# Start-up loads, the openings of two attention stages and one matmul order in a sixteen-stage network

## The chip, the core and the metric

The kernel runs on one core of a Trainium2 chip. The metric is the device time of one execution in microseconds (us), as the median of several; lower is better. The core has five engines with a queue of instructions each: TensorE (PE; its weight loads are the rows PEld), VectorE (DVE), ScalarE (ACT), GpSimd (POOL) and SyncE (SP, which here issues most DMAs). The engines meet only at semaphores: an instruction raises one when it is done (`then_inc`), and another engine's queue waits for a value of it (`wait_ge`).

## The reference, cut to what matters

Sixteen layers in a row, each `x = x + layer(layernorm(x))`, over a batch of 4 blocks of 512 positions with 128 features. The layers that the change touches compute this:

```python
# L0 and L3 "attn_a" (Mamba): conv of 4 taps over time, then a scan over time with 16 states
xc = sum(x_pad[:, k:k + Lln, :] * conv_w[:, k] for k in range(D_CONV)) + conv_b
h = A_bar * h + dt_t[..., None] * B_t[:, None, :] * x_t[..., None]
# L0 and L2 "attn_b" (narrow attention): 16 heads of 8 features, softmax over all keys (L2: causal)
score = softmax(einsum('bhif,bhjf->bhij', q, k) / SCALE); attn = einsum('bhij,bhjf->bihf', score, v)
# L1 "ffn": weights given as booleans, +1 or -1
w = jnp.where(kernel_bool, 1.0, -1.0)
# L1 "attn_b" (wide attention): 16 heads of 64 features, softmax, output projection
logits = einsum('bhne,bhme->bhnm', q, k); out = einsum('bhnm,bhme->bnhe', softmax(logits), v)
# L3 "attn_b" (ReLU attention): one score per head and position, standardised over time, then
# context of i = 2 * sum_j relu(z_i - z_j) * v_j / norm, by sorting in the reference
# L3 "ffn": integer weights, times 1/127
h = jax.nn.silu(gate) * up
```

## The kernel before, in words

The loop `Fori` in `network` runs two passes, each over two of the four blocks (`NB = 2`). Features lie on the 128 partitions, the 512 positions of a block along the free axis; `g.xs` holds x for both blocks through a whole pass. A pass is a chain of stages (`L0a`, `L0f`, ... `L3g`), each a `Block` of its own: no engine begins a stage before all of them have ended the one before. Within a stage the order on each engine is written out by hand. Banks 0 to 7 of `g.ps` are PSUM.

- `prepare` (L139) loads all 15,793 weight columns in eight pieces on SP, then the booleans and the integers, and on DVE makes the ternary matrix (L167 to L178), the +1/-1 matrices `g.conn` (L182 to L187) and the scaled integers `g.gated` (L192, L194). POOL folds the input projection into the conv taps of both Mamba layers in place (L207) and halves their output matrices (L208). 
- `load_x` and `store_x` (L220, L233) are stages of their own around a pass: one DMA of two blocks each, waited for.
- `mamba` begins with the norms on ACT and DVE; the first convolution (L985) follows the prepared input `xin`.
- `narrow_attention` (L0b, L2b) cuts q and k in bf16 parts. For each group of heads it first finds the row maxima: PE makes a score tile (`top_scores`, L1536), DVE takes its maximum (L1737; causal L1734). 17 such steps make a unit of a block and four heads (the 17th turns the maxima, L1530). Three PSUM banks go round: a score tile waits until DVE has done the one three before. Beside that run 64 slots: PE makes the real scores (`scores`, L1549), ACT their exponential (L1649), and in every second slot PE multiplies with the values (`products`, L1566). Each slot also holds 2 or 3 of the maxima's score tiles.
- `wide_attention` (L1b) projects k, q and v for a pair of heads (L1832, L1835), and in 64 steps makes scores (L1846), maxima on DVE (L1979), exponentials on ACT (L1942), transposes on PE (L1857) and products (L1869); the output projection of a block is L1889. All projections pass through one bank, `SMALL`, so that each waits for ACT to have copied the one before.
- `relu_attention` (L3b) makes z for queries and keys of both blocks (x = 2b the queries, 2b + 1 the keys), standardises it, cuts the queries in three bf16 parts (`split_q`), and then in 8 units u spreads four query rows over all partitions (`spread`, L2153), copies them (ACT, L2265), and makes relu(z_i - z_j) for four key tiles, three on DVE (L2415) and one on ACT (L2285), which PE multiplies with the values (L2197). Units 0 to 3 are block 0, units 4 to 7 block 1.

## Time and profile before

| | |
|---|---|
| median of 3 runs | 3164.71 us (3163.57 to 3168.61) |
| the profiled execution | 3165.05 us, its span 3163.5 us |
| PE busy | 2570.9 us (81%) |
| DVE busy | 1586.3 us (50%) |
| ACT busy | 1446.3 us (46%) |
| POOL busy | 677.6 us (21%) |
| DMA | 55.68 MB, 18 GB/s on average |

The span is the time from the first to the last instruction that the profiler recorded; what lies around it is 1.55 us here. In a row of the timeline the number in front is the start in us from the span's start, the second the duration; "x4" is how many instructions the row merges, and the bracket says how long the engine had been idle before it and what ended that.

### The profile page before, as it was taken

How to read it: one execution, taken by the hardware profiler on the slowest of the kernel's cores; microseconds unless marked ns; L12 is line 12 of the kernel's file. 1: busy time of each engine (PE TensorE's matmuls, PEld its weight loads, DVE VectorE, ACT ScalarE, POOL GpSimd, SP SyncE). 2: the span in 40 equal slices, each digit the busy share in tenths (PEclk: the TensorE clock that was granted, in tenths of full speed). 3: DMA queues.
4: the chain of work that ended last, by engine and by line, in shares of the span. 5: the costliest groups of instructions: out<-in, count | busy, mean ns of one | idle time of the engine just before them, and what ended most of it. 6: DMA issues, size and time to landing. Idle time of an engine off the chain costs nothing. (4 is left out here: it accounts for less than half of the span.)

```text
span 3163.5 us, 33520 instructions
## 1 busy us (share of the span) xinstructions
PE 2570.9 (81%) x11730; PEld 1095.1 (35%) x11738; DVE 1586.3 (50%) x2507; ACT 1446.3 (46%) x2392; POOL 677.6 (21%) x644
## 2 busy tenths in 40 slices
PE   3777788999789789768767787889997897897677
PEld 1231244544344234223222213445443442342232
DVE  3967543555121631695649585245442117217955
ACT  3544614555334354554545355155552444445454
POOL 1732010000001521371227311000000024115520
PEclk9898989999979899899889989999998898998998
DMA  3002000000010210000000010000000102100000
GB/s 122 1 1 73 8 1 1 1 1 1 1 53 1 76 59 0 0 1 1 1 15 1 25 56 1 1 1 1 1 1 0 53 1 81 54 0 1 0 1 7
DMA packets 36751, 55.68 MB, mean 18 GB/s; under 512 B 7648, under 2 KB 19936, under 8 KB 36576
## 3 DMA queue, kind: packets, MB, share of 16 engines
q1 hardware_dynamic: 32224, 49.53, 4.8%
q10 hardware_dynamic: 4352, 3.94, 0.4%
q8 instruction: 96, 1.57, 0.2%
q14 instruction: 79, 0.65, 0.1%
HBM read 39.54 MB, written 13.63 MB: 17 GB/s over the span
## 5 line engine op out<-in xcount | busy, mean ns | idle before, releaser
L522 POOL TENSOR_TENSOR xs<-xs,L2f_part 128x512 f32<-128x512 f32 x32 | 40.5, 1264 | 1181.8 <-DVE L2f_part L511 1181.8
L1942 ACT ACTIVATE L1b_pr<-ps,L1b_mneg 128x512 f32<-128x512 f32 x256 | 173.7, 684 | 197.0 <-DVE L1b_mneg L1981 197.0
L1979 DVE TENSOR_REDUCE L1b_m<-ps 128x2 f32<-128x1024 f32 x128 | 156.8, 1225 | 114.9 <-PE ps L1846 111.2
L1649 ACT ACTIVATE L0b_pt<-ps 128x1024 f32<-128x1024 f32 x128 | 129.3, 1024 | 117.9 <-PE ps L1549 115.8
L90 ACT ACT_TABLE_LOAD x44 | 56.5, 1283 | 268.0 <-PEq L224 41.4
L1737 DVE TENSOR_REDUCE L0b_mx<-ps 128x1 f32<-128x512 f32 x256 | 159.0, 684 | 37.0 <-PE ps L1536 35.5
L1226 POOL TENSOR_TENSOR L3a_db<-L3a_du,L3a_bs 128x1024 f32<-128x1024 f32 x64 | 150.4, 2360 | 114.0 <-DVE L3a_du L1337 68.1
L1226 POOL TENSOR_TENSOR L0a_db<-L0a_du,L0a_bs 128x1024 f32<-128x1024 f32 x64 | 150.5, 2359 | 112.5 <-DVE L0a_du L1337 66.0
L2005 DVE COPY L1b_prt<-ps 128x512 f32<-128x512 f32 x128 | 88.5, 692 | 124.9 <-PE ps L1857 124.6
L1354 DVE TENSOR_TENSOR_SCAN L0a_hs<-ps,L0a_db 128x1024 f32<-128x1024 f32 x64 | 146.1, 2283 | 5.4 <-ACT ps L1149 5.4
L1354 DVE TENSOR_TENSOR_SCAN L3a_hs<-ps,L3a_db 128x1024 f32<-128x1024 f32 x64 | 146.1, 2282 | 5.0 <-ACT ps L1149 5.0
L1846 PE MATMUL ps<-L1b_k,L1b_q 64*128 64x512 f32 x512 | 145.3, 646 | 0.0
L115 PE MATMUL ps<-xs,weights 128*128 128x512 f32 x128 | 79.5, 753 | 78.8 <-PEq L224 31.3
L1869 PE MATMUL ps<-L1b_prt,L1b_v 128*64 128x512 f32 x512 | 136.7, 614 | 4.1 <-issue 2.0
L1857 PE MATMUL ps<-weights,L1b_pr 128*128 128x128 f32 x1024 | 135.8, 275 | 3.0 <-ACT L1b_pr L1942 3.0
L1649 ACT ACTIVATE L2b_pt<-ps 128x1024 f32<-128x1024 f32 (+3 forms) x128 | 86.9, 706 | 105.5 <-PE ps L1549 104.8
L1857 PEld LDWEIGHTS ps<-weights,L1b_pr 128*128 128x128 f32 x1024 | 115.6, 141 | 50.6 <-issue 43.5
L1036 PE MATMUL ps<-L0a_hc,weights 128*128 128x512 f32 x256 | 127.5, 625 | 5.1 <-ACT L0a_du L1129 3.0
L511 DVE SCALAR_TENSOR_TENSOR L2f_part<-ps,weights,L2f_masks 128x512 f32<-128x512 f32 x32 | 24.1, 752 | 206.0 <-PE ps L443 206.0
L1036 PE MATMUL ps<-L3a_hc,weights 128*128 128x512 f32 x256 | 123.2, 608 | 5.1 <-ACT L3a_du L1129 3.0
L511 DVE SCALAR_TENSOR_TENSOR L2g_part<-ps,weights,L2g_masks 128x512 f32<-128x512 f32 x32 | 24.1, 752 | 202.0 <-PE ps L443 202.0
L1734 DVE CUSTOM_DVE_ANT_0 L2b_unmasked<-ps,weights 128x128 bf16<-128x128 f32 (+3 forms) x256 | 110.0, 488 | 30.4 <-PE ps L1536 27.3
(566 smaller groups left out, 5274.2 us busy)
## 6 DMA issues: line engine op xcount, KB each, us to landing
L2f_w<-expert_dram SPq DMA_DIRECT2D x32, 256.0 KB, 3.0
L2g_w<-expert_dram SPq DMA_DIRECT2D x32, 256.0 KB, 3.0
weights<-w_dram SPq DMA_DIRECT2D x7, 987.5 KB, 10.7
L0b_qs<-stack_dram SPq DMA_DIRECT2D x32, 96.0 KB, 2.2
stack_dram<-L0b_cut SPq DMA_DIRECT2D x24, 128.0 KB, 2.1
L2b_qs<-stack_dram SPq DMA_DIRECT2D x32, 96.0 KB, 2.2
stack_dram<-L2b_cut SPq DMA_DIRECT2D x24, 128.0 KB, 2.2
L0b_ks<-stack_dram SPq DMA_DIRECT2D x28, 96.0 KB, 2.2
```

What stands on the lines that cost most here:

```text
L1036: mm = pe.matmul(g.ps[:, SUM + k, :], g.w("ident"), hc[:, n % DEEP, k, :], start=(s == 0), stop=(s == NS - 1))
L1226: pool.tensor_tensor(db[:, n % DEEP, :, :], du[:, b, :, :], bcast(bs[:, n % DEEP, :], 1, 2), ALU.mult).then_inc(input_ready, 1)
L1354: dve.tensor_tensor_scan(flat(hs), decay_banks(n).rearrange("p k t -> p (k t)"), flat(db), 0.0, ALU.mult, ALU.add).then_inc(scanned, 1)
L1649: act.activation(pt[:, n % 3, 2 * half:2 * half + 2, q0:T], g.ps[:, 2 * (s % 2):2 * (s % 2) + 2, q0:T], ACT.Exp).then_inc(prob, 1)
L1734: dve.tensor_tensor_reduce(unmasked[:, e % 3, 0:span(t)], g.ps[:, bank, 0:span(t)], g.w("causal_row", T - span(t)), 1.0, -3e38, ALU.add, A ...
L1737: dve.tensor_reduce(mx[:, u, col:col + 1], g.ps[:, bank, 0:T], AX.X, ALU.max).then_inc(top_in, 1)
L1846: mm = pe.matmul(g.ps[:, 2 * (s % 2) + h, :], q[HE * h:HE * h + HE, u % 3, t * P:(t + 1) * P], k[HE * h:HE * h + HE, u % 3, :], start=True ...
L1857: mm = pe.transpose(g.ps[:, 4 + h, j * P:(j + 1) * P], pr[:, s % 2, h, j * P:(j + 1) * P], g.w("ident"))
L1869: mm = pe.matmul(g.ps[HE * h:HE * h + HE, PV, :], v[:, u % 4, j, HE * h:HE * h + HE], prt[:, u % 2, h, j, :], start=(j == 0), stop=(j == K ...
L1942: act.activation(pr[:, s % 2, h, :], g.ps[:, 2 * (s % 2) + h, :], ACT.Exp, bias=mneg[:, s % 2, h:h + 1], accum_out=total[:, u % 2, t, h:h ...
L1979: dve.tensor_reduce(m[:, s % 2, :], g.ps[:, 2 * (s % 2):2 * (s % 2) + 2, :], AX.X, ALU.max).then_inc(max_raw, 1)
L2005: dve.tensor_copy(prt[:, u % 2, 0, :, t * P:(t + 1) * P], g.ps[:, 4, :].rearrange("p (j c) -> p j c", c=P)).then_inc(turned_dve, 1)
```

## The change

What is different now, in five parts:

1. **Start.** The weights are sorted by need. SP loads 1013 columns, then x of the first pass, then 3551 columns (the rest that layer L0a needs), then the others in six pieces, which only the second stage waits for. The conversion of the booleans moves to POOL in L1a, that of the integers to POOL in L1b; both are done in each pass. The folding of the taps moves to POOL at the start of each Mamba stage, into the memory of `dt`'s second block.
2. **Turn.** `load_x` and `store_x` go. The last stage, L3g, puts its result in `g.xn` and issues for each block the store and the load of the next x into `g.xs`. A stage `close` without work stands at the end of a pass.
3. **Wide attention.** The six opening projections go to different banks; the first three wait for the first block's norm alone, and `scores(0)` comes after three of them. The last output projection goes to bank 4 and begins before the last pair is ready.
4. **ReLU attention.** Banks are spread; the queries and keys of block 0 are standardised in one instruction each, with the square of the queries on DVE; the rest of block 1's preparation is moved from between the units to before the first, and `spread(4)` from unit 2 to the end of unit 3.
5. **Narrow attention.** In a slot, the maxima's score tiles come before the products.

The diff, cut to its core:

```diff
-                for c in range(cut):
-                    a, z = c * step, min(n, (c + 1) * step)
-                    sp.dma_start(g.weights[:, a:z], wd[:, a:z]).then_inc(loaded, 16)
-                sp.dma_start(bools[:, :], boold).then_inc(bools_in, 16)
-                sp.dma_start(ints[:, :], intd).then_inc(ints_in, 16)
+                sp.dma_start(g.weights[:, 0:cut[0]], wd[:, 0:cut[0]]).then_inc(loaded, 16)
+                sp.dma_start(g.xs[:, :, :], x_dram[0:NB, :, :].rearrange("b p t -> p b t")).then_inc(x_loaded, 16)
+                sp.dma_start(g.weights[:, cut[0]:cut[1]], wd[:, cut[0]:cut[1]]).then_inc(loaded, 16)
+                for c in range(REST):
+                    a, z = (cut[1] + (n - cut[1]) * k // REST for k in (c, c + 1))
+                    sp.dma_start(g.weights[:, a:z], wd[:, a:z]).then_inc(g.rest_loaded, 16)
+                sp.wait_ge(x_loaded, 16)
...
-                dve.wait_ge(loaded, 16 * cut)
+                dve.wait_ge(loaded, 32)
...
+                dve.tensor_scalar(g.s2x[:, :], g.w("f1_s", 0, 2), 2.0, None, ALU.mult).then_inc(consts, 1)
+                dve.tensor_copy(g.cb[:, :], g.w("bf_consts")).then_inc(consts, 1)
...
-            @block.gpsimd
-            def _(pool):
-                pool.wait_ge(loaded, 16 * cut)
-                for name in ("m0", "m3"):
-                    rows = g.w(name + "_taps").rearrange("p (j e) -> p j e", j=4)
-                    pool.tensor_tensor(rows, rows, bcast(g.w(name + "_in", 0, 2 * P), 1, 4), ALU.mult).then_inc(taps, 1)
-                    pool.tensor_scalar(g.w(name + "_out"), g.w(name + "_out"), 0.5, None, ALU.mult).then_inc(taps, 1)
...
+                if last:
+                    for b in range(NB):
+                        sp.wait_ge(added, b + 1)
+                        sp.dma_start(out_dram[bass.ds(i * NB + b, 1), :, :].rearrange("b p t -> (b p) t"), g.xn[:, b, :]).then_inc(stored, 16)
+                        sp.dma_start(g.xs[:, b, :], x_dram[bass.ds(NB + b - i * NB, 1), :, :].rearrange("b p t -> (b p) t")).then_inc(x_loaded, 16)
...
-                    dve.tensor_tensor(g.xs[:, b, :], g.xs[:, b, :], g.ps[:, 4 * b + 3, :], ALU.add).then_inc(added, 1)
+                    dve.tensor_tensor(result[:, b, :], g.xs[:, b, :], g.ps[:, 4 * b + 3, :], ALU.add).then_inc(added, 1)
...
+                pool.wait_ge(bools_in, 16)
+                pool.tensor_copy(g.conn[:, :], bools[:, FF:]).then_inc(conn_steps, 1)
...
+                pool.tensor_tensor(g.conn[:, 0:FF], ahead[:, :], g.conn[:, 0:FF], ALU.subtract).then_inc(conn_steps, 1)
...
+                pool.tensor_scalar(g.conn[:, FF:], g.conn[:, FF:], 2.0, 1.0, ALU.mult, ALU.subtract).then_inc(conn_steps, 1)
...
+                        pe.wait_ge(folded, 2)
...
+                        mm = pe.matmul(g.ps[:, CONV[b] + f, :], taps[:, j, f * P:(f + 1) * P], xin[:, b, j:j + T], start=(j == 0), stop=(j == 3))
...
+                rows = g.w(w + "_taps").rearrange("p (j e) -> p j e", j=4)
+                pool.tensor_tensor(taps[:, :, :], rows, bcast(g.w(w + "_in", 0, 2 * P), 1, 4), ALU.mult).then_inc(folded, 1)
+                pool.tensor_scalar(out_w[:, :], g.w(w + "_out"), 0.5, None, ALU.mult).then_inc(folded, 1)
...
-                    if s >= LAG and (s - LAG) % 2 == 0:
-                        products((s - LAG) // 2)
                     for a in range(tops_before(s), tops_before(s + 1)):
                         top_scores(e, a)
                         e += 1
+                    if s >= LAG and (s - LAG) % 2 == 0:
+                        products((s - LAG) // 2)
                     c = (s - TURN) // 16
...
+        OPENING = (SMALL, PV, 4, 5, SMALL, PV)
+        def proj_bank(u, j):
+            return OPENING[3 * u + j] if u < 2 else SMALL
...
+                pool.wait_ge(ints_in, 16)
+                pool.tensor_copy(g.gated[:, :], ints[:, :]).then_inc(gated_steps, 1)
...
+                pool.tensor_scalar(g.gated[:, :], g.gated[:, :], 1.0 / 127.0, None, ALU.mult).then_inc(gated_steps, 1)
...
+                        else:
+                            pe.wait_ge(proj_in, 3 + h)
...
+                    if b == NB - 1:
+                        bank = LAST
...
+                    else:
+                        pe.wait_ge(at_ready, PAIRS * (b + 1))
...
+                        mm = pe.matmul(g.ps[:, bank, :], g.w("w1_wp", p * P, P), at[:, b % 2, p, :], start=(p == 0), stop=(p == PAIRS - 1))
...
 
+                pe.wait_ge(ln.done, 1)
+                for j in range(3):
+                    project(0, j)
+                scores(0)
+                project(1, 0)
                 pe.wait_ge(ln.done, NB)
-                for u in range(2):
-                    for j in range(3):
-                        project(u, j)
-                scores(0)
                 for s in range(STEPS):
                     u, t = s // KT, s % KT
                     if s + 1 < STEPS:
                         scores(s + 1)
+                    if s == 0:
+                        project(1, 1)
+                        project(1, 2)
...
-                for u in range(2):
-                    for j in range(3):
-                        take(u, j)
+                for j in range(3):
+                    take(0, j)
+                take(1, 0)
                 exps(0)
+                take(1, 1)
+                take(1, 2)
...
-                    if x >= 2:
-                        pe.wait_ge(turned_in, x - 1)
...
+                    if x == 2:
+                        pe.wait_ge(v_in, 2)
...
-                    if x == 1:
-                        pe.wait_ge(z_in, 1)
...
-                    pe.wait_ge(z_ready, b + 1)
-                    pe.wait_ge(z_in, 2 * b + 2)
+                    pe.wait_ge(k_ready, b + 1)
+                    pe.wait_ge((v_in, hid_in)[b], (1, XS)[b])
...
-                turn(3)
-                hide(2)
-                hide(3)
                 turn_keys(0)
...
-                        pe.wait_ge(turned_in, XS)
                         pe.wait_ge(hid_in, 2)
+                        pe.wait_ge(z_in, 2)
...
+                turn(3)
+                hide(2)
+                hide(3)
+                scores(2)
+                scores(3)
                 spread(1)
                 for n in range(4 * UN):
                     b, i, t = n // 16, n // 4 % 4, n % 4
-                    if n == 2:
-                        scores(2)
-                        scores(3)
-                    if n == 11:
+                    if n == 15:
+                        spread(4)
                         turn_keys(1)
-                    if t == 2 and n // 4 + 2 < UN:
+                    if n == 16:
+                        spread(5)
+                    if t == 2 and n // 4 + 2 < UN and n // 4 not in (2, 3):
                         spread(n // 4 + 2)
...
+                    if n == 8:
+                        pe.wait_ge(z_in, XS)
...
-                    act.wait_ge(z_c, x + 1)
-                    act.activation(ln.xc[:, x % 2, :], z[:, x, :], ACT.Square, accum_out=sums[:, x, 1:2]).then_inc(z_sq, 1)
...
+                    act.activation(ln.xc[:, x % 2, :], z[:, x, :], ACT.Square, bias=minus[:, x:x + 1], accum_out=sums[:, x, 1:2]).then_inc(z_sq, 1)
...
-                square(0)
...
-                take_turned(3)
-                gelu(2)
-                gelu(3)
...
+                take_turned(3)
+                gelu(2)
+                gelu(3)
+                take_z(2)
+                take_z(3)
+                load_exp_ln(g.nc)
...
-                    if u + 1 < UN:
+                    if u + 1 < UN and u != 3:
                         take_q(u + 1)
+                    if u == 1:
+                        square(2)
+                        square(3)
...
-                    if u == 0:
-                        take_z(2)
-                        take_z(3)
-                        load_exp_ln(g.nc)
                     if u == 1:
-                        square(2)
-                        square(3)
                         inverse_std(1)
-                    if u == 2:
+                    if u == 3:
+                        take_q(4)
                         take_keys(1)
...
+                def scale_k(b):
+                    x = 2 * b + 1
...
+                    pool.tensor_scalar(z[:, x, :], z[:, x, :], minus[:, x:x + 1], std[:, b:b + 1], ALU.add, ALU.mult).then_inc(k_ready, 1)
...
-                        pool.tensor_scalar(z[:, 1, :], z[:, 1, :], std[:, 0:1], None, ALU.mult).then_inc(z_ready, 1)
...
                     pool.wait_ge(z_in, x + 1)
-                    pool.tensor_scalar(sums[:, x, 2:3], sums[:, x, 0:1], 1.0 / T, None, ALU.mult).then_inc(z_mean, 1)
...
-                    pool.tensor_scalar(z[:, x, :], z[:, x, :], sums[:, x, 2:3], None, ALU.subtract).then_inc(z_c, 1)
-                pool.wait_ge(z_sq, 4)
+                    pool.tensor_scalar(minus[:, x:x + 1], sums[:, x, 0:1], -1.0 / T, None, ALU.mult).then_inc(z_mean, 1)
+                pool.wait_ge(z_sq, 3)
                 pool.tensor_tensor(var[:, 1:2], sums[:, 2, 1:2], sums[:, 3, 1:2], ALU.add).then_inc(z_var, 1)
-                pool.wait_ge(z_std, 2)
-                for x in (3, 2):
-                    pool.tensor_scalar(z[:, x, :], z[:, x, :], std[:, 1:2], None, ALU.mult).then_inc(z_ready, 1)
-                split_q(pool, z_ready, 1)
+                split_q(pool, 1)
+                pool.wait_ge(lo, 2)
+                scale_k(1)
...
-                centre_z(1)
+                mean_z(0)
+                dve.wait_ge(z_mean, 1)
+                dve.tensor_scalar(ln.xc[:, 0, :], z[:, 0, :], minus[:, 0:1], None, ALU.add).then_inc(z_c, 1)
...
+                dve.tensor_tensor_reduce(ln.sq[:, 0, :], ln.xc[:, 0, :], ln.xc[:, 0, :], 1.0, 0.0, ALU.mult, ALU.add, sums[:, 0, 1:2]).then_inc(q_sq, 1)
+                mean_z(1)
                 take_rows(2)
-                dve.wait_ge(z_sq, 2)
+                dve.wait_ge(z_sq, 1)
+                dve.wait_ge(q_sq, 1)
                 dve.tensor_tensor(var[:, 0:1], sums[:, 0, 1:2], sums[:, 1, 1:2], ALU.add).then_inc(z_var, 1)
+                scale_q(0)
+                split_q(dve, 0)
                 take_rows(3)
                 take_v(1)
-                dve.wait_ge(z_std, 1)
-                dve.tensor_scalar(z[:, 0, :], z[:, 0, :], std[:, 0:1], None, ALU.mult).then_inc(q_ready, 1)
...
-                split_q(dve, q_ready, 0)
...
-                    if u % 4 == 2:
+                    if u == 1:
+                        scale_q(1)
+                    if u == 2 or u == 5:
...
-            load_x(g, x_dram, i)
...
+    first = ("f0_w", "f0_alpha", "f0_b", "f1_s", "bf_consts", "mean_mat", "m0_alog", "m3_alog")
+    early = first + ("centre", "ident", "eps5", "eps6")
+    rank = lambda name: 0 if name in first else 1 if name in early or name.startswith("m0_") else 2
+    parts.sort(key=lambda part: rank(part[0]))
+    cut = [sum(m.shape[1] for name, m in parts if rank(name) <= k) for k in range(2)]
```

On PE, in the slots of L0b, L1536 (now L1532) are the maxima's score tiles, L1549 (L1545) the real scores and L1566 (L1562) the products. Before:

```order
L1549 MATMUL ps<-L0b_qs,L0b_ks 128x512 x2
L1566 MATMUL ps<-L0b_pt,L0b_vpad 32x512 x4
L1536 MATMUL ps<-L0b_ks,L0b_qs 128x512 x2
L1549 MATMUL ps<-L0b_qs,L0b_ks 128x512 x2
L1536 MATMUL ps<-L0b_ks,L0b_qs 128x512 x2
L1549 MATMUL ps<-L0b_qs,L0b_ks 128x512 x2
L1566 MATMUL ps<-L0b_pt,L0b_vpad 32x512 x4
L1536 MATMUL ps<-L0b_ks,L0b_qs 128x512 x2
```

Now:

```order
L1545 MATMUL ps<-L0b_qs,L0b_ks 128x512 x2
L1532 MATMUL ps<-L0b_ks,L0b_qs 128x512 x2
L1562 MATMUL ps<-L0b_pt,L0b_vpad 32x512 x4
L1545 MATMUL ps<-L0b_qs,L0b_ks 128x512 x2
L1532 MATMUL ps<-L0b_ks,L0b_qs 128x512 x2
L1545 MATMUL ps<-L0b_qs,L0b_ks 128x512 x2
L1532 MATMUL ps<-L0b_ks,L0b_qs 128x512 x2
L1562 MATMUL ps<-L0b_pt,L0b_vpad 32x512 x4
```

The four products of a slot stand behind the two score tiles where they stood ahead of them.

On PE, in the opening of L1b, L1832 and L1835 (now L1847 and L1850) are projections, L1846 (L1861) scores and L1857 (L1874) transposes of the exponentials. Before:

```order
L1832 MATMUL ps<-xn,weights 128x512 x2
L1835 MATMUL ps<-weights,xn 128x128 x4
L1832 MATMUL ps<-xn,weights 128x512 x2
L1835 MATMUL ps<-weights,xn 128x128 x4
L1846 MATMUL ps<-L1b_k,L1b_q 128x512 x4
L1857 MATMUL ps<-weights,L1b_pr 128x128 x8
```

Now:

```order
L1847 MATMUL ps<-xn,weights 128x512 x2
L1850 MATMUL ps<-weights,xn 128x128 x4
L1861 MATMUL ps<-L1b_k,L1b_q 128x512 x2
L1847 MATMUL ps<-xn,weights 128x512
L1861 MATMUL ps<-L1b_k,L1b_q 128x512 x2
L1847 MATMUL ps<-xn,weights 128x512
L1850 MATMUL ps<-weights,xn 128x128 x4
L1874 MATMUL ps<-weights,L1b_pr 128x128 x8
```

The first scores stand behind three projections instead of six, and the other three stand around the second.

On PE, in the opening of L3b, L2103 (now L2133) turn the rows, L2109 (L2141) and L2116 (L2146) are the two layers behind z, L2123 (L2153) turns the keys, L2153 (L2180) spreads queries and L2197 (L2231) are products. Before:

```order
L2094 MATMUL ps<-weights,L3b_xm 128x128 x4
L2103 MATMUL ps<-weights,L3b_rows 128x128 x8
L2109 MATMUL ps<-L3b_rt,weights 128x512 x2
L2123 MATMUL ps<-weights,L3b_z 128x16 x4
L2153 MATMUL ps<-L3b_zc,cb 128x512 x8
L2197 MATMUL ps<-L3b_re,L3b_vpad 32x512 x8
L2116 MATMUL ps<-L3b_hid,weights 128x512 x2
L2153 MATMUL ps<-L3b_zc,cb 128x512 x4
```

Now:

```order
L2126 MATMUL ps<-weights,L3b_xm 128x128 x4
L2133 MATMUL ps<-weights,L3b_rows 128x128 x4
L2153 MATMUL ps<-weights,L3b_z 128x16 x4
L2180 MATMUL ps<-L3b_zc,cb 128x512 x4
L2133 MATMUL ps<-weights,L3b_rows 128x128 x4
L2141 MATMUL ps<-L3b_rt,weights 128x512 x2
L2146 MATMUL ps<-L3b_hid,weights 128x512 x2
L2180 MATMUL ps<-L3b_zc,cb 128x512 x4
L2231 MATMUL ps<-L3b_re,L3b_vpad 32x512 x8
```

The first spread of queries stands ahead of the fourth turn and the hidden layers; the second-layer matmuls of block 1 stand before the first product instead of in the first unit.

## Rows read from the trace of the kernel before

**Rows 1.** Windows: busy us and count per engine, granted clock, DMA share, GB/s
```profile
560.00:760.00 200.00, 197.87 (x1118) 99.97 (x1117) 108.78 (x169) 115.02 (x286) 0.00 (x0) 1.00 0.00 1
265.60:351.50 85.90, 69.31 (x419) 15.30 (x418) 68.97 (x116) 53.76 (x54) 5.88 (x18) 0.94 0.15 43
```

**Rows 2.** Timeline of the start: start us, us, engine line op, idle before
```profile
0.80 4.14 SPq L159 DMA_DIRECT2D weights<-w_dram  x8
...
22.55 0.29 DVE L167 TENSOR_REDUCE prep_absum<-weights 128x1 f32<-128x128 f32 x1 [22.55 <-DMA weights<-w_dram]
...
28.08 1.98 DVE L182 CAST conn<-prep_bools 128x3072 f32<-128x3072 uint8 x1
...
39.93 3.60 PE L115 MATMUL ps<-xs,weights 128*128 128x512 f32 x4 [16.45 <-PEq L224]
...
50.16 8.77 PE L985 MATMUL ps<-L0a_xin,weights 128*128 128x512 f32 x16 [4.82 <-DVE L0a_xin L1283]
```

**Rows 3.** DMA issues of the first 40 us: count, KB each, median us to landing
```profile
weights<-w_dram SPq DMA_DIRECT2D x7, 987.5 KB, 10.7
...
xs<-x_dram SPq DMA_DIRECT2D x1, 512.0 KB, 3.7
```

**Rows 4.** Timeline of the turn between the two passes
```profile
1591.03 0.69 DVE L378 TENSOR_TENSOR xs<-xs,ps 128x512 f32<-128x512 f32 x1 [1.89 <-PE ps L354]
1592.92 0.41 SPq L239 DMA_DIRECT2D out_dram<-xs  x1
1601.30 0.42 SPq L229 DMA_DIRECT2D xs<-x_dram  x1
...
1605.85 1.28 ACT L90 ACT_TABLE_LOAD   x1 [24.68 <-PEq L224]
```

**Rows 5.** Timeline of the wide stage's opening (L1b)
```profile
501.80 1.13 PE L1832 MATMUL ps<-xn,weights 128*128 128x512 f32 x2 [2.55 <-DVE xn L136]
...
516.26 2.68 PE L1846 MATMUL ps<-L1b_k,L1b_q 64*128 64x512 f32 x8
...
520.43 1.32 PE L1857 MATMUL ps<-weights,L1b_pr 128*128 128x128 f32 x8 [1.49 <-ACT L1b_pr L1942]
```

**Rows 6.** Window of that opening
```profile
504.00:518.00 14.00, 11.25 (x28) 5.48 (x28) 0.00 (x0) 2.99 (x5) 0.00 (x0) 0.51 0.00 0
```

**Rows 7.** Timeline of the wide stage's end
```profile
782.49 7.13 PE L1889 MATMUL ps<-L1b_at,weights 128*128 128x512 f32 x16 [1.22 <-DVE L1b_at L1987]
```

**Rows 8.** Maxima of the narrow stages, engine idle until: L0b 265.6:351.5, L2b 1064.9:1128
```profile
  PE ps L1536: 12.4, 25
  PE ps L1536: 8.7, 13
```

**Rows 9.** Timeline of two slots of L0b
```profile
312.64 2.48 DVE L1737 TENSOR_REDUCE L0b_mx<-ps 128x1 f32<-128x512 f32 x4 [0.73 <-PE ps L1536]
...
313.92 1.07 PE L1566 MATMUL ps<-L0b_pt,L0b_vpad 128*32 128x512 f32 x8
```

**Rows 10.** Timeline of the ReLU stage (L3b)
```profile
1486.41 1.57 POOL L2316 TENSOR_SCALAR L3b_z<-L3b_z,L3b_std 128x512 f32<-128x512 f32 x1 [5.89 <-ACT L3b_std L2232]
...
1489.16 0.48 DVE L2384 TENSOR_SCALAR L3b_z<-L3b_z,L3b_std 128x512 f32<-128x512 f32 x1
...
1495.72 4.84 DVE L2415 TENSOR_SCALAR L3b_re<-L3b_qb,L3b_zk 128x512 f32<-128x512 f32 x12 [3.11 <-ACT L3b_qb L2265]
...
1515.33 3.41 DVE L2415 TENSOR_SCALAR L3b_re<-L3b_qb,L3b_zk 128x512 f32<-128x512 f32 x4
...
1520.49 1.89 PE L2153 MATMUL ps<-L3b_zc,cb 128*128 128x512 bf16 x4 [7.26 <-POOL L3b_zc L2065]
```

**Rows 11.** Timeline of the linear stage (L1a), GpSimd and end
```profile
406.33 6.20 POOL L842 TENSOR_SCALAR L1a_km<-L1a_k,weights 128x512 f32<-128x512 f32 x4 [8.84 <-DVE L1a_k L853]
...
417.19 2.45 POOL L829 COPY L1a_vpad<-L1a_v 128x32 f32<-128x32 f32 x16 [4.66 <-ACT L1a_v L788]
...
444.85 0.75 DVE L909 SCALAR_TENSOR_TENSOR xs<-ps,weights,xs 128x512 f32<-128x512 f32 x1 [1.22 <-PE ps L772]
```

171 lines of the change are left out of this document (89 added, 82 removed).

## The prediction, made before the changed kernel ran

> **What bounds the kernel now.** I read the windows of busy time first. In the wide stage L1b PE works 197.87 of 200 us at granted clock 1.00 [rows 1]: PE sets its length, and what is taken from its opening comes off in full. In the narrow stage L0b nothing is full: PE 69.31 and DVE 68.97 of 85.90 us. They wait for each other, and only a count of those waits says what a new order can give. So next I read by which instruction DVE was released in the maxima: it stood idle for score tiles 12.4 us in 25 places of L0b and 8.7 us in 13 of L2b [rows 8]. Last come the timelines of places where every engine waits: the start, the turn and the openings of L1b and L3b [rows 2, 4, 5, 10]. There a row's bracket names what ended the wait. Stages do not overlap, so a saving inside one reaches the end at full size if it shortens that stage's last chain, and counts twice if it is not in the start or the turn.
>
> **Start.** DVE does nothing until 22.55, when the last of eight weight pieces (8.09 MB, 15,793 columns of 512 bytes) has landed; at 28.08 its ternary steps are over and the conversions begin; L0a's first matmul is at 39.93 [rows 2]. Now DVE waits for 1013 + 3551 columns with x between them: 0.52 + 0.52 + 1.82 = 2.86 MB. The eight issues took 4.14 us from 0.80, 0.52 each, so the fourth was over near 2.9 and issued near 2.6; the median landing is 10.7 us after an issue [rows 3], so 4.04 MB was there at about 13.3. From there to 22.55 runs 0.44 MB per us; the 1.18 MB less than 4.04 makes 2.7 us less: 10.6. The ternary steps took 28.08 - 22.55 = 5.5 us, with POOL folding beside them; that folding leaves the stage, so I take 3 to 5.5. The small casts add under 0.5 (by columns of the 1.98 us cast: 688 / 3072 x 1.98). Then the change of stage, 1.20 us as in the turn (1591.72 to 1592.92) [rows 4]. L0a begins near 15.3 instead of 39.9: **-24.6**, bounds -20 (pieces land late) to -27. The load of x and its stage, 35.77 on, are inside that figure. The folding now stands in L0a, on POOL, ahead of the first convolution at 50.16, 10.2 us into the stage [rows 2]; the two instructions took under 3.9 us beside DVE in preparation, an upper bound from the 5.5 us there. Cover: 6 us; without it, 3.9 us per Mamba stage. Cost 0.
>
> That the pieces land in the order of issue is my choice. The Trainium skill (DMA: Bandwidth & Descriptors, Queues, rings and completion order) says completion is not first in, first out even though descriptors are taken in ring order. No row shows single landings; if it mixes them, this is the second rival below.
>
> **Turn.** From the last sum (1591.72) to the next L0a (1605.85) pass 14.13 us: 1.20 to the store, 8.38 from store to load, 4.55 from load to first work [rows 4]. Of these 4.55, 3.7 is the landing [rows 3]. Now store and load of a block are issued behind its own sum, two DMAs each at 0.42, the first pair hidden under the second block; the last pair lands near 1595.5. Behind it stand two changes of stage (L3g to `close`, `close` to the loop), 1.2 each, and the loop itself, which is what the 8.38 leaves beyond a landing of 3.7: 4.7. Total 1595.5 + 1.2 + 4.7 = 1601.4, to 1602 with the empty stage: **-3.5 to -4**, I take -3.5; bounds -5 and 0. At the kernel's end a load nobody needs runs beside the store: 0 to +1, taken 0.
>
> **Wide opening (L1b), each pass.** Now the first projection starts at 501.80 after 2.55 us idle for the second block's norm; each later projection of the six waits for ACT's copy of the one before, and the first scores stand at 516.26, with the clock at 0.51 from 504 to 518 [rows 5, 6]. In the changed order the first three projections have banks of their own and wait for block 0's norm alone, at the earliest 499.25, so I take 500.6. Three at 1.13 end at 504.0; scores to transposes took 520.43 - 516.26 = 4.17, so transposes begin at 508.2, 12.2 earlier. The other three projections (1.13 each) still have to be done, beside the first exponentials, when PE waits 1.49 for ACT in any case; of the 3.4 us I count 2.7 as exposed. **-9.5**. Lower bound: the clock stays low as in rows 6 while PE does the steps pulled ahead; they run at half speed, and half of 9.5 is left, -4.8. Upper: -11, all three hidden. ACT has three copies in the way of its exponentials rather than none: in the 2.7. At the end the output projection starts without its 1.22 us wait for the last pair [rows 7]: **-1.2**. The conversion of integers on POOL falls where POOL is idle: 200 us of the stage show no row of it [rows 1]. Cost 0. Two passes: 2 x (-10.7) = **-21.4**.
>
> **Narrow stages, each pass.** A period of two slots holds about four maxima of 0.62 us (2.48 for four) and four products of which eight take 1.07 [rows 9]; DVE waits 0.73 there for a score tile while PE does products. With tiles ahead, DVE's banks are refilled first and products of some 0.5 to 1.06 us run while it reduces. Limits: 12.4 and 8.7 if every wait vanishes [rows 8], 0 if ACT's exponentials, 53.76 of 85.90 busy, or PE's own 69.31 come next. The tiles also need maxima three back, which is the wait that now stands ahead of the products. PE has 16.6 us free in that window, so I take three quarters in L0b, **-9**. In L2b, where the causal masks and DMA loads come between, only **-2**. Two passes: **-22**, bounds 0 and -42.
>
> **ReLU opening (L3b), each pass.** The keys' scaling ran on POOL 1486.41 to 1487.98; the queries' on DVE only at 1489.16, behind block 1's rows; the first differences began at 1495.72 [rows 10]. Queries now start when the deviation is there: 2.75 us from 1486.41 to 1489.16. A second square leaves ACT's chain; no row here has its price, I take 0.65, near DVE's 0.69 for 512 columns [rows 4]. Later, PE waited 7.26 us for block 1's split on POOL [rows 10]; that preparation now begins before unit 0 and that wait should mostly close. Against it: turn, GELU and z of block 1, two matmuls each and a table load of 1.28 [rows 4] stand on ACT ahead of unit 1's copies, and DVE has 3.11 us waits for such a copy already. With four copies at 0.65 the load makes 3.9. First start -3.4, split -4, unit 1 late +3.9: **-3.5**; bounds +4 (the delay alone, split still late) and -10.7 (3.4 + 7.26). Two passes: **-7**.
>
> **Conversions on POOL in L1a.** POOL is idle 8.84 before 406.33; four 512-column instructions take 6.20, so 1.55 per 512 or 3.0 ns a column; the last values are placed at 419.64 [rows 11]. Five instructions over 7168 columns cost 21.9 at that rate: over at 441.5, against the stage's last addition ending at 445.60. Cover 4.1 us; at one and a half times that rate the stage ends about 7 us later, in both passes (+14). I take 0.
>
> Here DVE's speed is at stake too. Four of its differences took 3.41 us beside POOL's split against 0.40 each (12 in 4.84) without [rows 10]. Work of 0.40 that takes 0.85 loses half its rate, so 21.9 us of conversion could cost up to 11 us of DVE's work in each pass. DVE mostly reads PSUM in L1a, so my sum holds nothing for it; the fourth rival does. The Trainium skill (GPSIMD Engine Reference, § 8 Key points) has GpSimd share its SBUF interface with VectorE: by that rule both conversions are at odds with DVE, and the trace agrees with its 0.85.
>
> **Sum.** -24.6 - 3.5 - 21.4 - 22 - 7 = -78.5. It is made against the profiled execution, 3165.05 (span 3163.5 and 1.55 around it), which stands 0.34 above the median of 3164.71: 3086.5, or 3086.2 by the median. Forecast 3086.5.
>
> **Rivals.** First, *orders give little*: L1b's opening half (-12 in all), ReLU nothing, of the narrow stages -5 in each L0b, start and turn whole: -24.6 - 3.5 - 12 - 10 = -50, **3115**. For it: PE and DVE in L0b are both near 80% busy, so a wait closed may open next door. Against: 25 waits of DVE are named for exactly these tiles. Second, *pieces land together*: x and the early columns share the queues with the rest, and DVE starts near 22.55 as before; then L0a begins at 22.55 + 3.9 + 0.5 + 1.2 = 28.1, which is -11.8 for -24.6: **3099**. Against: seven pieces have a median of 10.7, half of the time of the last, so they do not end together. Third, the other side, *the narrow order serialises*: with tiles ahead, the products wait behind a tile that waits for a maximum, ACT then waits for its bank or buffer behind them, and each of 32 periods in four stages shows PE's 1.06 of products in full: +136 for -22, so 3165 - 56.5 + 136 = **3245**. It decides once ACT is later than DVE in a period; against it, 53.76 of ACT to 68.97 of DVE. Fourth, *the moved work is not hidden*: the clock stays at 1.2 GHz through L1b's opening (+4.7 each), and POOL overruns L1a or slows DVE there (+7 each): 3086.5 + 9.4 + 14 = **3110**. For it, 0.85 beside 0.40 [rows 10] and 0.51 in rows 6; against, DVE's cover in L1a is PSUM work.
>
> **How the numbers follow.** Chances: forecast 0.60, first rival 0.15, second 0.10, fourth 0.08, third 0.04, and 0.03 for something near no change. What this kernel's measurement can tell from no change is 0.2%, 6.3 us. The four that gain make faster 0.93; same 0.02; slower 0.05. The forecast's own bounds do not all fall to one side: 3062 has narrow at its full 42 (-20), L1b's opening at 11 (-3) and the turn at -5, 3125 has narrow and ReLU at nothing (+29) and the clock low in L1b (+9.4). I leave the third rival out: 3062 to 3125.
>
> **What would show it.** Right: first L0a matmul between 14 and 19; L0a to L0a of the turn near 10.5; L1b's first transposes about 12 us into the stage, its 64 steps unchanged; DVE's idle for tiles in L0b under 4 us; last GpSimd row of L1a before the last sum. Wrong: a first weight landing near 22; a clock near 0.5 well past L1b's scores; ACT idle for PE products in L0b; DVE waiting over 5 us for z or its deviation in L3b's unit 1 or 2; DVE rows in L1a longer than before.

## The result, and the profile after

| | before | changed |
|---|---|---|
| median | 3164.86 us (4 runs, 3163.57 to 3168.61) | 3094.11 us (4 runs, 3084.67 to 3098.29) |
| ratio, changed to before | | 0.977, 95% interval 0.9746 to 0.9794 |
| profiled execution, its span | 3165.05, 3163.5 us | 3098.29, 3096.7 us |

The changed kernel is 70.8 us faster by the medians and 66.8 us by the two spans; forecast were 78.5. The execution that was profiled is the slowest of the four. The top of its page:

```profile
span 3096.7 us, 33560 instructions
...
PE 2560.1 (83%) x11738; PEld 1095.2 (35%) x11738; DVE 1578.2 (51%) x2505; ACT 1440.3 (47%) x2388; POOL 709.2 (23%) x656
```

Since stages do not overlap, the span can be cut where they begin and compared piece by piece (us). A piece begins with the first instruction that names a tile of the stage's own; up to 2.1 us of a stage's opening (a table load, the first matmuls of its norm) stand before that and are counted with the piece before it:

| piece | before, pass 1 / 2 | changed, pass 1 / 2 | difference | forecast |
|---|---|---|---|---|
| start to L0a | 39.89 | 12.93 | -26.96 | -24.6 |
| L0b | 147.56 / 147.82 | 138.80 / 138.71 | -8.76 / -9.11 | -9 each |
| L1a | 64.20 / 64.18 | 63.69 / 63.79 | -0.51 / -0.39 | 0 |
| L1b | 295.38 / 295.39 | 281.78 / 281.77 | -13.60 / -13.62 | -10.7 each |
| L2b | 120.24 / 120.07 | 126.62 / 126.73 | **+6.38 / +6.66** | -2 each |
| L3b | 105.00 / 104.63 | 105.46 / 104.77 | **+0.46 / +0.14** | -3.5 each |
| L3g to next L0a (turn) | 37.14 | 32.17 | -4.97 | -3.5 |

The rest, -2.5 us, lies in stages that the change hardly touches, and differs by as much from pass to pass (L2f 128.42 and 125.71 in the changed kernel). Cut at the very first instruction of each stage instead, L2b goes from 118.95 and 117.95 to 124.50 and 124.60: 0.8 us of the +6.38 lie in the opening of the stage behind it.

The start and the turn, in the timeline of the changed kernel, against [rows 2, 4] (start us, duration, engine, line, operation, idle before and what ended it):

```profile
0.80 0.41 SPq L154 DMA_DIRECT2D weights<-w_dram  x1
...
9.99 0.29 DVE L166 TENSOR_REDUCE prep_absum<-weights 128x1 f32<-128x128 f32 x1 [9.99 <-DMA weights<-w_dram]
...
12.18 0.29 DVE L179 TENSOR_SCALAR tern<-tern,weights 128x128 f32<-128x128 f32 x1
...
12.91 3.75 PE L116 MATMUL ps<-xs,weights 128*128 128x512 f32 x4 [2.00 <-PEq L151]
12.93 2.35 POOL L1209 TENSOR_TENSOR L0a_dt<-weights 128x1024 f32<-128x1024 f32 x1 [12.42 <-POOLq L151]
...
1548.53 0.69 DVE L351 TENSOR_TENSOR xn<-xs,ps 128x512 f32<-128x512 f32 x1 [1.89 <-PE ps L327]
1549.39 0.35 SPq L306 DMA_DIRECT2D out_dram<-xn  x1
1550.05 0.34 SPq L307 DMA_DIRECT2D xs<-x_dram  x1
1558.27 3.78 PE L116 MATMUL ps<-xs,weights 128*128 128x512 f32 x4 [9.77 <-issue]
```

The first pieces are there at 9.99, not 22.55, and the ternary steps take 2.48 us from there, not 5.5. Their last instruction is one and the same; before, it ran beside POOL's folding:

```profile
25.75 2.41 DVE L178 TENSOR_SCALAR tern<-tern,weights 128x128 f32<-128x128 f32 x1
```

At the turn 9.3 us pass from the last sum (1549.22) to the row of L0a at 1558.53 (its first matmul is at 1558.27), not 14.13.

The opening of L1b, against [rows 5, 6]; the window is the same stretch of the stage (7.4 to 21.4 us after its start):

```profile
464.20 1.99 PE L1847 MATMUL ps<-xn,weights 128*128 128x512 f32 x4 [1.31 <-DVE xn L137]
...
467.01 1.13 PE L1861 MATMUL ps<-L1b_k,L1b_q 64*128 64x512 f32 x4
...
471.14 1.05 PE L1850 MATMUL ps<-weights,xn 128*128 128x128 f32 x8
472.04 1.04 PE L1874 MATMUL ps<-weights,L1b_pr 128*128 128x128 f32 x8
```
```profile
467.64:481.64 14.00, 13.49 (x69) 7.17 (x66) 8.56 (x12) 9.87 (x25) 0.13 (x1) 1.00 0.01 1
```

PE runs without a gap from the first projection to the transposes, which begin 11.78 us into the stage (before, 23.81), and the granted clock is 1.00 (2.4 GHz) where it was 0.51 (nearly all of it at the lower level, 1.2 GHz). All six projections are done by then. The windows of the whole stage, before and changed, pass 1:

```profile
496.62:792.00 295.38, 281.11 (x1513) 139.90 (x1512) 146.99 (x228) 161.31 (x392) 0.00 (x0) 0.98 0.00 1
```
```profile
460.26:742.04 281.78, 274.90 (x1513) 137.70 (x1512) 147.11 (x228) 161.20 (x392) 4.27 (x2) 1.00 0.01 3
```

The same 1513 matmuls keep PE busy 6.21 us less, and its idle time falls from 14.27 to 6.88 us, by 7.39. Together these are the 13.60.

L0b's maxima, the engine's idle until a score tile came (us, times), against [rows 8]:

```profile
L1733 DVE TENSOR_REDUCE L0b_mx<-ps x103: 680/681/693, 237.9 to 314.7; 128x1 f32<-128x512 f32 x103
...
  PE ps L1532: 3.4, 10
```

And what PE waited for in all of L2b, pass 1 (us in total, times, longest): changed, then before.

```profile
PE ps L1526 <- DVE L2b_mx L1730: 6.5, 6, 1.3
PE ps L1532 <- DVE L2b_mx L1730: 5.9, 18, 0.5
...
PE ps L1526 <- DVEq L1757: 2.1, 2, 1.1
```
```profile
PE ps L1536 <- DVE L2b_mx L1734: 6.0, 20, 0.4
PE ps L1530 <- DVE L2b_mx L1734: 4.0, 6, 1.2
```

L1526 (before, L1530) is the transposition of a unit's maxima. It waits for the maximum that was just asked for, and now the products are behind it: 6.5 + 2.1 us instead of 4.0 + 1.0 (the row L1530 <- DVEq L1761, further down in the view of before). The plain tiles wait as before. The windows of the whole stage show the other part of the loss, PE's granted clock (the column ahead of the last two); before, then changed, pass 1, then changed, pass 2:

```profile
1031.13:1151.37 120.24, 90.76 (x595) 29.78 (x596) 73.57 (x289) 52.63 (x78) 53.57 (x103) 0.84 0.19 54
```
```profile
981.19:1107.81 126.62, 93.89 (x595) 32.06 (x596) 73.61 (x289) 51.82 (x79) 54.02 (x103) 0.80 0.18 51
2524.68:2651.41 126.73, 95.73 (x595) 32.08 (x596) 73.65 (x289) 51.94 (x79) 54.00 (x103) 0.77 0.18 51
```

In pass 1 the +6.38 are 3.25 us more idle time of PE (29.48 to 32.73) and 3.13 more of busy time for the same 595 matmuls; in pass 2 the +6.66 are 1.15 (29.85 to 31.00) and 5.51 (90.22 to 95.73). A mean clock between 0.50 and 1.00 is a mix of the two levels.

L3b of the changed kernel, against [rows 10]:

```profile
1448.41 4.84 DVE L2457 TENSOR_SCALAR L3b_re<-L3b_qb,L3b_zk 128x512 f32<-128x512 f32 x12 [1.79 <-ACT L3b_qb L2295]
...
1456.62 1.88 ACT L2295 ACTIVATE L3b_qb<-ps 128x2048 f32<-128x2048 f32 x1
...
1458.53 1.68 DVE L2457 TENSOR_SCALAR L3b_re<-L3b_qb,L3b_zk 128x512 f32<-128x512 f32 x4 [5.27 <-ACT L3b_qb L2295]
...
1467.71 8.07 DVE L2457 TENSOR_SCALAR L3b_re<-L3b_qb,L3b_zk 128x512 f32<-128x512 f32 x12
```

The first differences begin 27.5 us into the stage, 4.5 sooner than before (32.0). Then DVE stands for 5.27 us until ACT has the copy for unit 1, and twelve differences of unit 2, beside POOL's split, take 8.07 us where twelve took 4.84. Slow differences and a long stand of DVE at the end of the block are not new in themselves; before, there were these, the second behind PE's wait of 7.26 us for the split:

```profile
1504.82 9.99 DVE L2415 TENSOR_SCALAR L3b_re<-L3b_qb,L3b_zk 128x512 f32<-128x512 f32 x20 [2.02 <-PE ps L2197]
...
1524.31 5.01 DVE L2415 TENSOR_SCALAR L3b_re<-L3b_qb,L3b_zk 128x512 f32<-128x512 f32 x12 [5.57 <-PE ps L2197]
```

Of L1a, POOL's last and longest conversion and the stage's last addition, against [rows 11]:

```profile
389.89 8.85 POOL L833 TENSOR_SCALAR conn<-conn 128x2560 f32<-128x2560 f32 x1
...
408.68 0.75 DVE L898 SCALAR_TENSOR_TENSOR xs<-ps,weights,xs 128x512 f32<-128x512 f32 x1 [1.22 <-PE ps L750]
```

The five ran from 383.65 to 398.74: 15.1 us, with 10 us to spare before the last addition.

### The profile page after: what moved, and what is told of

Same layout as the page of the kernel before. It is cut to its first block and busy times, and to the rows that moved or that the text cites. A ratio compares the mean times of both kernels' runs of the same rounds, so it can differ in the third digit from the quotient of the medians.

```text
span 3096.7 us, 33560 instructions
## 1 busy us (share of the span) xinstructions
PE 2560.1 (83%) x11738; PEld 1095.2 (35%) x11738; DVE 1578.2 (51%) x2505; ACT 1440.3 (47%) x2388; POOL 709.2 (23%) x656
## 5 line engine op out<-in xcount | busy, mean ns | idle before, releaser
L1222 POOL TENSOR_TENSOR L0a_db<-L0a_du,L0a_bs 128x1024 f32<-128x1024 f32 x64 | 150.5, 2361 | 105.7 <-DVE L0a_du L1333 60.9
L1222 POOL TENSOR_TENSOR L3a_db<-L3a_du,L3a_bs 128x1024 f32<-128x1024 f32 x64 | 150.4, 2360 | 105.7 <-DVE L3a_du L1333 60.5
L2036 DVE COPY L1b_prt<-ps 128x512 f32<-128x512 f32 x128 | 88.5, 692 | 126.3 <-PE ps L1874 126.0
L1861 PE MATMUL ps<-L1b_k,L1b_q 64*128 64x512 f32 x512 | 144.5, 641 | 0.0
L1874 PE MATMUL ps<-weights,L1b_pr 128*128 128x128 f32 x1024 | 135.3, 274 | 0.0
L1874 PEld LDWEIGHTS ps<-weights,L1b_pr 128*128 128x128 f32 x1024 | 115.8, 140 | 45.5 <-issue 43.5
## 6 DMA issues: line engine op xcount, KB each, us to landing
weights<-w_dram SPq DMA_DIRECT2D x3, 936.0 KB, 15.3
```

The source lines that it names most:

```text
L1222: pool.tensor_tensor(db[:, n % DEEP, :, :], du[:, b, :, :], bcast(bs[:, n % DEEP, :], 1, 2), ALU.mult).then_inc(input_ready, 1)
L1861: mm = pe.matmul(g.ps[:, 2 * (s % 2) + h, :], q[HE * h:HE * h + HE, u % 3, t * P:(t + 1) * P], k[HE * h:HE * h + HE, u % 3, :], start=True ...
L1874: mm = pe.transpose(g.ps[:, 4 + h, j * P:(j + 1) * P], pr[:, s % 2, h, j * P:(j + 1) * P], g.w("ident"))
L2036: dve.tensor_copy(prt[:, u % 2, 0, :, t * P:(t + 1) * P], g.ps[:, 4, :].rearrange("p (j c) -> p j c", c=P)).then_inc(turned_dve, 1)
```

## The experiments

x1 to x7 are the changed kernel with one edit each, x8 to x10 with several. Beside them, on the same chip, the kernel before took 3160.88 us (x1 to x4), 3163.20 (x5 to x8) and 3162.61 (x9, x10). Most stages repeat far better than the whole time, so the stages of the trace decide; the medians, with the ratio to the kernel before and its 95% interval, are given beside them. The line numbers in an experiment's rows are its own, a few off those above.

**x1_l2b_old**

```diff
-                    for a in range(tops_before(s), tops_before(s + 1)):
+                    due = s >= LAG and (s - LAG) % 2 == 0
+                    if due and causal:
+                        products((s - LAG) // 2)
+                    for a in range(tops_before(s), tops_before(s + 1)):
...
-                    if s >= LAG and (s - LAG) % 2 == 0:
+                    if due and not causal:
                         products((s - LAG) // 2)
```

> The changed kernel, with the products ahead of the maxima's score tiles again in the causal stage L2b alone; L0b keeps the new order. Theory A: the new order itself made L2b longer (120.24 to 126.62 us in the first pass, 120.07 to 126.73 in the second): both passes return to 120 to 120.5, L0b stays at 138.8, the span is near 3084. Rival B: L2b is longer because the clock or the loads fell differently there, whatever the order: it stays near 126.6 and the span near 3097.

Measured: 3081.42 us (ratio 0.9747, 0.9731 to 0.9764), 12.7 below the changed kernel's median, or 7 by the two ratios. L2b is 119.92 in pass 1 and 123.11 in pass 2, L0b 137.92 and 138.76. The order made L2b longer: theory A. Pass 2 lies outside A's range, though its code is that of pass 1. The windows of the two passes show the difference:

```profile
974.73:1094.65 119.92, 90.14 (x595) 29.55 (x596) 73.61 (x289) 52.63 (x79) 53.74 (x103) 0.85 0.19 54
```
```profile
2510.86:2633.97 123.11, 93.65 (x595) 30.87 (x596) 73.67 (x289) 52.85 (x78) 53.73 (x103) 0.81 0.18 53
```

The same 595 matmuls are busy 93.65 us and not 90.14, with the clock at 0.81 and not 0.85; DVE's and POOL's work is the same. So with the old order L2b is 120 or 123 by the clock it gets. With the new one it is 126.0 to 129.4 in 15 of the 16 passes profiled, and 123.3 in one, pass 1 of x8 below:

```profile
978.74:1102.00 123.26, 90.69 (x595) 30.77 (x596) 73.63 (x289) 51.90 (x79) 53.83 (x103) 0.83 0.18 53
```

There PE is busy as long as before the change (90.69, 90.76), and the stage is 3.0 us longer by PE's idle time alone. That is the price of the order where the clock does not fall with it. In the other 15 passes PE is idle 30.3 to 33.7 us and busy 93.1 to 99.1, so the clock takes half of the loss or more in most of them.

**x2_turn_late**

```diff
+                    due = s >= LAG and (s - LAG) % 2 == 0
                     for a in range(tops_before(s), tops_before(s + 1)):
+                        if due and a % 17 == 16:
+                            products((s - LAG) // 2)
+                            due = False
                         top_scores(e, a)
                         e += 1
-                    if s >= LAG and (s - LAG) % 2 == 0:
+                    if due:
                         products((s - LAG) // 2)
```

> The changed kernel, with one thing moved in both narrow stages: where a slot holds the transposition of a unit's maxima, it and what follows it come behind the slot's products; all other score tiles stay ahead of them. Theory A1: the loss of L2b is this transposition, which waits for the maximum just before it (up to 1.27 us) with the products queued behind: L2b falls from 126.6 to 121 or less, and L0b by 0 to 2 from 138.8. Rival A2: it is the plain tiles, each waiting for its bank with products behind: L2b stays within 1.5 of 126.6.

Measured: 3085.99 us (0.9763, 0.9746 to 0.9779). L2b is 120.87 and 123.25, within 1 us of the old order; L0b is 138.88 and 138.78, unchanged. A1 holds in L2b (pass 2 lies above its 121, at a clock of 0.81): of the whole new order, it is the transposition ahead of the products, with the tiles behind it in its slot, that costs. PE's waits for it are near the old ones again:

```profile
PE ps L1526 <- DVE L2b_mx L1734: 3.7, 5, 1.2
```

With its two waits in the row L1526 <- DVEq L1761, 1.2 us, that is 4.9 us instead of 8.6. In pass 1 PE's idle time falls by 2.7 us (32.73 to 30.01) and its busy time by 3.0 (93.89 to 90.86, clock 0.80 to 0.83); the stage gains 5.75. In L0b nothing more came. The maxima are longer there (0.68 us each, in L2b 0.29 to 0.69), and DVE was short of tiles for 3.4 us only; that this is the reason is not shown.

**x7_l0b_old** has the edit of x1 with `causal` and `not causal` exchanged, so that only L0b has the old order.

> The changed kernel, with the products ahead of the maxima's score tiles again in L0b alone; L2b keeps the new order. Theory I, the order alone gave L0b's 8.8 to 9.1 us: L0b is 147 to 148 in both passes and DVE's waits for the tiles are back, L2b stays at 126.6. Rival J, something else in the change (the clock, the loads) did: under 143.

Measured: 3110.84 us (0.9829, 0.9813 to 0.9846). L0b is 147.97 and 148.43, L2b 126.66 and 128.81 (126.6 expected for both). DVE's waits for the tiles are back to 12.3 us in 25 places:

```profile
  PE ps L1532: 12.3, 25
```

Theory I holds: the order alone is worth about 9 us for each L0b.

**x3_six**

```diff
-                pe.wait_ge(ln.done, 1)
-                for j in range(3):
-                    project(0, j)
-                scores(0)
-                project(1, 0)
                 pe.wait_ge(ln.done, NB)
+                for u in range(2):
+                    for j in range(3):
+                        project(u, j)
+                scores(0)
...
-                    if s == 0:
-                        project(1, 1)
-                        project(1, 2)
...
-                for j in range(3):
-                    take(0, j)
-                take(1, 0)
+                for u in range(2):
+                    for j in range(3):
+                        take(u, j)
                 exps(0)
-                take(1, 1)
-                take(1, 2)
```

> The changed kernel, with the old order in the opening of L1b (all six projections, then the first scores, ACT's six copies ahead of its first exponentials) on the new banks. L1b is 281.8 us in the changed kernel and 295.4 before. Theory C, the banks gave most of it (no wait for a copy between projections, and so a clock of 1.00 there): L1b is 285 to 287, the projections without idle, the clock at 1.00. Rival D, the order gave most: 290 to 293.

**x4_onebank**

```diff
-        OPENING = (SMALL, PV, 4, 5, SMALL, PV)
+        OPENING = (SMALL,) * 6
...
-                    elif u == 1 and j >= 1:
-                        pe.wait_ge(proj_in, j)
+                    elif u + j >= 1:
+                        pe.wait_ge(proj_in, 3 * u + j)
```

> The changed kernel, with all six opening projections of L1b in one bank again, each waiting for ACT's copy of the one before, in the new order. Theory C, the banks gave most: idle of about 0.7 us ahead of five projections is back, the clock falls near 0.5 in the opening, L1b is 288 to 292. Rival D, the order gave most: L1b is 283 to 285.

Measured: x3 3101.81 us (0.9807, 0.9791 to 0.9823), L1b 286.05 and 284.36; x4 3099.58 us (0.9804, 0.9782 to 0.9825), L1b 284.63 in both passes. The order undone costs 2.6 to 4.3 us and the banks undone 2.9. Both together are undone in the kernel before, whose L1b is 13.6 us longer, 12.0 of it ahead of the first transposes. So C is wrong for x4 and D for x3: neither part gave most. Either part alone keeps most of the clock. The first 20 us of L1b, before, x3 and x4:

```profile
496.62:516.62 20.00, 14.02 (x32) 6.18 (x32) 1.39 (x2) 6.95 (x12) 0.00 (x0) 0.69 0.00 0
```
```profile
457.56:477.56 20.00, 15.96 (x60) 7.75 (x58) 6.48 (x10) 10.92 (x22) 4.27 (x2) 0.91 0.09 30
```
```profile
456.10:476.10 20.00, 16.35 (x64) 7.07 (x62) 7.18 (x11) 12.22 (x26) 4.26 (x2) 1.00 0.09 30
```

Before, with one bank and six projections in a row, PE waits 0.69 us for ACT ahead of five of them and the clock is granted at 0.69 over these 20 us: 32 matmuls get done. With either half of the change it is 60 or 64, at 0.91 or 1.00. Over the whole stage PE is idle 9.6 us in x3 and 8.9 in x4, where it is 6.9 in the changed kernel and 14.3 before; busy it is 276.4 and 274.7 (the two passes of x3) and 275.7, where it is 274.9 and 281.1. So what either half alone loses is waits, but for pass 1 of x3 (286.05, clock 0.99 over the stage), and most of the clock's 6.2 us is lost only with both undone. The expectation for x4 had five waits of 0.7 us and a clock near 0.5; there were three of 0.69, and the clock stayed at 1.00.

**x6_start_all**

```diff
                 dve.wait_ge(loaded, 32)
+                dve.wait_ge(g.rest_loaded, 16 * REST)
```

> The changed kernel, with preparation waiting for all weight pieces instead of the first two; order and sizes of the loads, and where things are converted, stay. L0a begins at 12.93 us in the changed kernel, at 39.89 before. Theory G, the order of the loads gives what the bytes give: the last piece lands near 22 (8.6 MB), and L0a begins at 24.5 to 26, so 12 of the 27 us come from the order and 15 from the moved conversions and the load of x. Rival H, the wait matters little since the pieces land together: L0a begins before 18.

Measured: 3108.41 us (0.9819, 0.9803 to 0.9836); L0a begins at 26.82, and DVE at

```profile
23.88 0.29 DVE L167 TENSOR_REDUCE prep_absum<-weights 128x1 f32<-128x128 f32 x1 [23.88 <-DMA weights<-w_dram]
```

G is right in kind and 0.8 us short in size. The order of the loads is worth 13.9 us, and 13.1 come from what left preparation, the load of x included. The pieces land in the order in which they are issued; the DMA view of the changed kernel has their medians from issue to landing. With issues at 0.80, 1.26 and 1.72 the first three are there near 4.4, 5.8 and 9.9 us:

```profile
weights<-w_dram SPq DMA_DIRECT2D x3, 936.0 KB, 15.3
weights<-w_dram SPq DMA_DIRECT2D x3, 935.5 KB, 13.5
weights<-w_dram SPq DMA_DIRECT2D x1, 1775.5 KB, 8.2
xs<-x_dram SPq DMA_DIRECT2D x1, 512.0 KB, 4.5
weights<-w_dram SPq DMA_DIRECT2D x1, 506.5 KB, 3.6
```

**x5_z_between**

```diff
-                scores(2)
-                scores(3)
                 spread(1)
...
+                    if n == 2:
+                        scores(2)
+                        scores(3)
...
-                take_z(2)
-                take_z(3)
-                load_exp_ln(g.nc)
                 for u in range(UN):
...
+                    if u == 0:
+                        take_z(2)
+                        take_z(3)
+                        load_exp_ln(g.nc)
```

> The changed kernel, with the second layer of z for block 1 (two matmuls on PE, two copies and the table load on ACT) back between the units of L3b, behind unit 0's first products; its transposition and GELU stay ahead of the units. L3b is 105.0 us before and 105.5 changed, though its first differences begin 4.5 us sooner. Theory E, block 1's preparation ahead of unit 1 gives the gain back: ACT's copy for unit 1 comes 2 to 4 us sooner, L3b is 101 to 103. Rival F, the queries' split on POOL beside DVE bounds the middle of the stage whatever is ahead of it: within 1 us of 105.4.

Measured: 3086.89 us (0.9757, 0.9737 to 0.9776). L3b is 101.90 and 102.49. ACT's copies for units 0 and 1 now follow each other, and F falls:

```profile
1440.70 1.88 ACT L2296 ACTIVATE L3b_qb<-ps 128x2048 f32<-128x2048 f32 x1 [0.85 <-PE ps L2180]
...
1445.54 1.88 ACT L2296 ACTIVATE L3b_qb<-ps 128x2048 f32<-128x2048 f32 x1
```

The second begins 4.8 us after the first and not 10.2 (1446.43 to 1456.62 in the changed kernel).

**x8_later** moves `hide`, too, behind unit 0 (PE at n = 2), `scores` to n = 4, GELU behind ACT's unit 0, `take_z` ahead of its unit 1, squares and deviation behind it, and `scale_q(1)` behind the first four differences of unit 2.

> The changed kernel, with the whole hidden layer of block 1 in L3b behind the first units: GELU behind unit 0's difference on ACT, z ahead of unit 1's, the squares and the deviation behind it, the queries' scaling on DVE inside unit 2. Theory E: ACT's copy for unit 1 follows the first at once, so unit 1 begins 6 to 8 us sooner than in the changed kernel, and L3b is 97 to 100. Rival F, the split for unit 4 is then the late one (before the change PE waited 7.26 us for it): L3b is 103 or more, with PE or ACT waiting for it ahead of unit 4.

Measured: 3086.61 us (0.9758, 0.9741 to 0.9774), L3b 102.29 and 102.16: ACT's copy for unit 1 begins 28.7 us into the stage, 7 sooner than in the changed kernel as E has it (1.8 sooner than in x5), and the stage is as long as x5's. E's length was missed, and F's too. DVE has the deviation of block 1 45.4 us into the stage, in x5 after 43.6, and waits 3.29 us for it (4.51 in x5): what one chain gained the next gave back.

**x9_split_dve** is x5 with

```diff
-                split_q(pool, 1)
-                pool.wait_ge(lo, 2)
                 scale_k(1)
...
                     if u == 1:
                         scale_q(1)
+                        split_q(dve, 1)
```

> The run with z of block 1 between the units of L3b (L3b 101.9 and 102.5 us), with one more thing changed there: block 1's queries are split on DVE behind unit 1, not on POOL beside DVE's unit 2. Theory K, POOL's five instructions cost DVE more than they take off it: unit 2's twelve differences, 8.05 us beside the split, take 4.9, DVE takes on 2.8 for the split, so L3b changes by 0 to -1.5. Rival L, the twelve differences are long for another reason (they wait for products): they stay near 8 and L3b grows by 2 to 3.

Measured: 3087.98 us (0.9758, 0.9741 to 0.9776), L3b 102.75 and 102.14, against 101.90 and 102.49 of x5. The first half of K holds exactly, L falls:

```profile
1465.52 4.84 DVE L2457 TENSOR_SCALAR L3b_re<-L3b_qb,L3b_zk 128x512 f32<-128x512 f32 x12
```

Twelve differences take 4.84 us again, not 8.05. But the split costs DVE 3.2 us, from 1462.33 to 1465.49, which is what it had cost beside POOL (8.05 - 4.84). The gain of 0 to -1.5 did not come.

**x10_best** puts together x1 (L2b alone), x9, and this:

```diff
-                    if n == 15:
-                        spread(4)
+                    if n == 12:
                         turn_keys(1)
-                    if n == 16:
-                        spread(5)
-                    if t == 2 and n // 4 + 2 < UN and n // 4 not in (2, 3):
+                    if t == 2 and n // 4 + 2 < UN:
                         spread(n // 4 + 2)
...
-                    if u + 1 < UN and u != 3:
+                    if u + 1 < UN:
                         take_q(u + 1)
+                    if u == 3:
+                        take_keys(1)
...
-                    if u == 3:
-                        take_q(4)
-                        take_keys(1)
```

> All that the runs point to, together: the changed kernel with L2b's old order, z of block 1 between the units of L3b, its queries split on DVE, and the spread of unit 4's and 5's queries and block 1's keys back at the places that other units have. L2b 120 to 123, L3b 96 to 100 (ACT's copy for unit 4 no longer waits behind unit 3's last difference, where DVE idled 4.2 us, and PE waits for no split), L0b and L1b as changed: 3081.4 measured with L2b alone, less 5 to 8 for each L3b: near 3068, range 3062 to 3078. Against it: with the spread of unit 4 in unit 2 PE could wait for the split there, and L3b stays near 102: near 3075.

Measured: 3068.95 us (5 runs, 3063.51 to 3076.72; ratio 0.9708, 0.9689 to 0.9727), 25 us below the changed kernel by the medians, 20 by the two ratios. L3b is 98.48 and 98.74, L2b 123.00 and 120.43. In L3b the only difference from x9 is where unit 4's and 5's queries and block 1's keys stand, so that is worth 3.4 to 4.3 us; whether it needs DVE's early split was not run. DVE's wait ahead of unit 4, 4.2 us in x9, is gone:

```profile
1466.20 4.84 DVE L2456 TENSOR_SCALAR L3b_re<-L3b_qb,L3b_zk 128x512 f32<-128x512 f32 x12 [0.41 <-PE ps L2232]
...
1471.22 4.84 DVE L2456 TENSOR_SCALAR L3b_re<-L3b_qb,L3b_zk 128x512 f32<-128x512 f32 x12 [0.18 <-PE ps L2232]
```

## Why the prediction was right, and where not

The measured median lies 7.6 us above the forecast of 3086.5, inside its range. The sum of -78.5 came out as -66.8 in the traces, but five of its terms were off by 1.5 to 17 us and partly made up for each other: L2b and L3b came 24.6 us worse than forecast, start, turn and L1b 9.6 better, and L1a and the stages not in the sum 3.4 better. That the total is as near as it is, is partly luck.

- *Start, -24.6 for -27.0.* The mechanism was right, and each step came out shorter. The landing was at 9.99 and not 10.6. The ternary steps took 2.5 us, where the 15.3 of the forecast holds 3 (its lower value). The small casts, 0.5 there, ran inside them. The change of stage, put at 1.20 as in the turn, took 0.46. So L0a began at 12.9, earlier than the 14 to 19 that was to be the sign. The second rival (pieces land together) is refuted by x6. I had left the folding in L0a at nothing; POOL's 12.93 row of 2.35 us is early, and L0a is 0.2 us shorter, so that holds.
- *Turn, -3.5 for -5.0.* The mechanism was right and the term mis-sized, to the end of its bounds. Its own steps give more than was taken: from 1601.4 or 1602 to 1605.85 is 4.4 or 3.9, not "-3.5 to -4". Beyond that, L0a began 9.3 us after the last sum, where 9.7 to 10.3 were worked out; landing, changes of stage and loop share 7.9 us behind the last issue (1550.39 to 1558.27), and no run divides them.
- *Wide opening and end, -10.7 for -13.6 each.* The first transposes came 12.0 us sooner, near the 12.2 worked out, but by another way: the 12.2 kept the 4.17 us from scores to transposes that had run at the low clock, and at the full clock the other three projections fitted in as well. The step that failed is "of the 3.4 us I count 2.7 as exposed": all six projections were done before the first transposes, so nothing was left to pay. The remaining 1.6 fell behind the first transposes, with 1.2 forecast for the end. What the prediction saw as a risk only, the clock, was 6.2 of the 13.6 us: x3 and x4 each lose about 3 us and keep it nearly whole, and only the kernel with both undone loses it.
- *Narrow stages, -9 for -8.8 and -9.1 in L0b.* x7 ties it to the order; DVE's waits went from 12.4 to 3.4 us, and the stage took nearly all of it.
- *Narrow, -2 for +6.5 in L2b.* The failed step is the upper end of "bounds 0 and -42": that nothing could be lost as long as ACT does not come late. The third rival had the right mechanism, products behind something that waits for a maximum, but tied it to plain tiles and to ACT. x2 shows it is the 17th step, the transposition, which waits for DVE's latest result and not for the one three back. The wait costs 3 us where the clock stays (pass 1 of x8). Added to it is the clock, from 0.84 to 0.80 and from 0.85 to 0.77, 3.1 and 5.5 us, which the prediction did not price.
- *ReLU opening, -3.5 for +0.3.* The first part was right (4.5 for 3.4), the late unit 1 was in the sum at 3.9 and was larger: the copy for unit 1 came 35.7 us into the stage, before 33.2, although unit 0 began 4.5 sooner: 7.1 us of the lead were lost there. The step "split -4" failed: the 7.26 us wait of PE did go, but DVE, which had stood 5.57 us for it, stands 4.21 for block 1's keys ahead of unit 4, and 5.27 for the copy and 3.26 for the deviation before that; the split slows differences as it did before (3.2 us in twelve of them). The recorded sign of being wrong, over 5 us of DVE waiting for z or its deviation, named nearly the right place. x5 shows that the place of block 1's z matters (-3.6 and -2.3), x9 that the engine of the split does not, x10 that the late places of `spread(4)`, `spread(5)` and the keys did.
- *Conversions, 0.* Those of L1a took 15.1 us, not 21.9, and L1a's DVE rows are the same to 1 ns (683 against 682 for its most frequent one). In L3b twelve differences take 4.84 us without the split beside them (x9) and 8.05 with it (x5). The Trainium skill (GPSIMD Engine Reference, § 8 Key points) limits the contention of GpSimd and VectorE to VectorE's instructions in a 2-port mode or with two SBUF inputs; the prediction applied the rule to both conversions without that condition. The most frequent DVE row of L1a reads PSUM and one tile of SBUF, and there no run shows contention.

The fourth rival (clock low in the opening, POOL overrunning) came true in neither half. The other signs of being right were met: 11.78 us to L1b's transposes, 3.4 us of idle for tiles in L0b, and GpSimd done before L1a's last sum.

## What to carry to other kernels

When one engine's instructions are put ahead of others, ask for each what it waits for: a tile that reuses a bank of three rounds ago is safe to put first, and an instruction that needs the newest result of another engine belongs behind all work that is ready. The two looked alike in the code here, and the same order gained 9 us in one stage and lost 6 in the other. Work moved out of the middle of a stage into its opening has to be counted on the engine that paces the opening, all of it; and the wait that it removes should be followed to the next one. Compare stages by themselves: terms of both signs hide in a total that looks as forecast.

## What the runs showed of the chip that was not expected

- The same instructions of a stage take different times by the granted clock. L1a took 59.6 us at 0.96 and 63.8 at 0.88 in the two passes of one execution, that of x1 (63.7 to 64.2 at 0.88 before and changed), with PE idle 15.6 us in both:

```profile
348.08:407.69 59.61, 44.05 (x611) 29.11 (x612) 39.35 (x66) 15.66 (x25) 29.90 (x42) 0.96 0.03 9
```
```profile
1880.47:1944.23 63.76, 48.21 (x611) 32.61 (x612) 39.36 (x66) 15.66 (x25) 29.91 (x42) 0.88 0.03 9
```

That is 4 us that no edit in L1a made. Together with L2b's 3 us it may be part of the nearly 14 us between the fastest and the slowest execution of the changed kernel (3084.67 to 3098.29), where the kernel before spreads over 5, and over up to 10 beside the experiments; of the four only the slowest was profiled, so this is not shown. What sets the level at a stage's start was not settled: of the ten experiments' profiles, pass 1 of L1a took 59.6 to 60.5 us in six and 63.7 or more in four, pass 2 59.6 to 60.9 in three and 63.7 or more in seven, with the code of L1a the same in all.
- Five gaps of PE of 0.69 us, one ahead of each projection of L1b but the first, went with a clock at 0.51, and a gap-free start with 1.00. With three of them left (x4) it was 1.00 too; with none, but the old wait of 2.54 us ahead of the first projection (x3), it was 0.91 over the first 20 us in one pass and 1.00 in the other.
- POOL converts uint8 to fp32 at 0.9 ns a column (2.75 us for 3072) and runs a TENSOR_SCALAR with two operations at 3.5 (8.85 us for 2560): the rate of one form says little of another.
